# Projections over parts, wider products for the values of layer 2, and later masks in a four-layer attention kernel

## The reference

```python
# L0: LayerNorm, cross attention of 16 heads of 16, MLP 256 -> 1024 -> 256
q = (ln(x) @ q_w + q_b); k = ctx @ k_w + k_b; v = ctx @ v_w + v_b
x = softmax(q k^T / 4) v @ cproj_w + cproj_b + x;  x = x + mlp(ln(x))
# L1: queries from x; keys and values from concat([ctx, x]); key mask; RMSNorm and MLP
q = x @ q_w + q_b;  kv = concat([ctx, x], 1) @ kv_w + kv_b;  ...
# L2: two cross attentions over ctx, 16 heads of 128, one learnt key and value more per head
for j in (1, 2):
    h = ln_j(x);  qh, kh, vh = h @ wq_j + bq_j, ctx @ wk_j + bk_j, ctx @ wv_j + bv_j    # 256 -> 2048
    x = x + softmax([qh kh^T, qh bias_k] / sqrt(128)) [vh; bias_v] @ wo_j + bo_j
x = x + mlp(ln(x))                                                                     # "M2"
# L3: self attention ("L3s"), cross attention over ctx ("L3c"), 16 heads of 16, MLP
qkv = ln1(x) @ w_qkv + b_qkv;  scores = scores * mask - 10000 * (1 - mask);  ...
q = ln2(x) @ w_q + b_q;  kv = ctx @ w_kv + b_kv;  ...;  x = x + mlp(ln3(x))
```

## Time and profile before

| | us |
|---|---|
| Median of 3 runs | 1060.3 (1059.1 to 1060.75) |
| The profiled execution | 1061.92 |
| Its span (first to last instruction) | 1060.7 |
| TensorE busy | 1032.2 |
| VectorE, ScalarE, GpSimd busy | 714.9, 596.2, 601.7 |
| Idle time of TensorE in the span | 28.5 |

### The profile page before, as it was taken

How to read it: one execution, slowest core, us unless ns; L and a number is a source line. 1 busy time by engine, 2 the same in 40 slices (tenths; PEclk the granted TensorE clock), 3 DMA queues, 4 the chain that set the end, 5 groups by cost and what they waited for, 6 DMA issues and landing times.

```text
span 1060.7 us, 20845 instructions
## 1 busy us (share of the span) xinstructions
PE 1032.2 (97%) x8080; PEld 917.0 (86%) x8080; DVE 714.9 (67%) x1086; ACT 596.2 (56%) x1311; POOL 601.7 (57%) x627
## 2 busy tenths in 40 slices
PE   8999999999999999999999999999998999989988
PEld 7787888878888999999988999999998888778877
DVE  6987888899366565565567655665654378988751
ACT  6988788878633333223344223333226499999963
POOL 6874557465654344343287333553525689999860
PEclk9999999999999999999999999999999999999999
DMA  9200001000112222211130101110100000000000
...
DMA packets 33786, 40.71 MB, mean 38 GB/s; under 512 B 2111, under 2 KB 31257, under 8 KB 32025
## 3 DMA queue, kind: packets, MB, share of 16 engines
...
...
## 4 chain that ended last, share of the span: by engine, by line
PE 74%; POOL 8%; DVE 8%; ACT 5%; issue 5%; POOLq 0%; DVEq 0%; ACTq 0%
PE psum L789 14%; PE psum L683 9%; PE psum L671 8%; PE psum L803 7%; PE psum L849 7%; PE psum L709 5%; PE psum L837 5%; PE psum L817 4%; PE psum L602 4%; PE psum L699 3%; PE psum L724 2%; POOL C tile L1565 2%; PE psum L826 2%; PE psum L656 2%; ACT C tile L1364 2%
## 5 line engine op out<-in xcount | busy, mean ns | idle before, releaser
L1658 POOL TENSOR_TENSOR B tile<-B tile,B rec 128x1024 f32<-128x1024 f32 x32 | 60.8, 1899 | 204.2 <-DVE B rec L1150 204.2
L1571 POOL TENSOR_TENSOR A tile<-A tile,outer rec 128x1024 f32<-128x1024 f32 x48 | 90.7, 1897 | 74.7 <-DVE outer rec L1039 74.7
L1426 ACT ACTIVATE B own<-B max 128x8 f32<-128x8 f32 x32 | 6.7, 209 | 163.9 <-DVE B tile L1137 163.9
L1364 ACT ACTIVATE A tile<-A tile,outer min 128x128 f32<-128x128 f32 (+1 forms) x256 | 92.3, 452 | 6.1 <-DVE outer min L1032 6.0
L1282 ACT ACTIVATE B kT<-psum,B bcol 128x1024 f32<-128x1024 f32 x32 | 35.7, 1117 | 91.6 <-PE psum L789 91.6
L1364 ACT ACTIVATE C tile<-C tile,outer min 128x128 f32<-128x128 f32 x256 | 78.0, 402 | 2.1 <-DVE outer min L1032 2.1
L1178 DVE TENSOR_TENSOR x_all<-x_all,psum 128x512 f32<-128x512 f32 x64 | 42.6, 685 | 54.3 <-PE psum L849 54.3
L803 PE MATMUL psum<-B v hi,B cT hi 128*128 128x256 f32 x256 | 74.1, 289 | 0.3 <-ACT B kT L1282 0.3
L803 PE MATMUL psum<-B v hi,B cT lo 128*128 128x256 f32 x256 | 72.4, 283 | 0.0
L803 PE MATMUL psum<-B v lo,B cT hi 128*128 128x256 f32 x256 | 72.4, 283 | 0.0
L930 DVE TENSOR_SCALAR B qT<-psum,B bcol 128x1024 f32<-128x1024 f32 x32 | 41.1, 1283 | 43.3 <-PE psum L789 43.3
...
## 6 DMA issues: line engine op xcount, KB each, us to landing
...
```

The lines of the kernel that those rows point to most:

```text
L1364: i = act.activation(of_head, of_head, ACT.Exp, bias=part.min[:, u % 4, h:h + 1], scale=-1.0)
L1571: pool.tensor_tensor(tile(u, ly.nk), tile(u, ly.nk), part.rec[:, u % 4, 0:ly.per].unsqueeze(2).to_broadcast([P, ly.per, ly.nk]), ALU.mult) ...
L1658: pool.tensor_tensor(tv, tv, m.brec[:, h, :].unsqueeze(2).to_broadcast([P, B, S]), ALU.mult).then_inc(s["normalised"].sem, s["normalised"] ...
```

## The change

1. **Projections over parts.** The `k` and `v` steps of L0, all `q`, `k`, `v` of L1 and L3s, and `k`, `v` of L3c, 48 steps in all, use three fp32r products where one float32 product stood. Only the `q` of L0 and of L3c stay. `ctx` is turned straight into its two parts at the start (ScalarE copies the high one, VectorE subtracts for the low one), and the later making of them at the end of stage A goes. The inputs of L1 and L3s get parts too: in L1 the one drain becomes a copy on ScalarE and a subtraction on VectorE, in L3s VectorE writes the normalised features, ScalarE copies and GpSimd subtracts. The weights are cut by `cut_weights`, on GpSimd but for L0's keys.
2. **Where splits are made.** M2's up weights are cut in turns 1 to 4 of j = 2, the last layer's up weights in the same turns behind the second division (before: in stage C); those of L3s's q, k and v in turns 5 to 7 ahead of the second division, those of L3c's k and v in turns 5 and 6 behind it.
3. **Values of layer 2.** In turns 2 to 5 a product is one batch x four heads (512 columns) for this turn and the next, 24 of them for half of the batches. Turn 1 has 24 products of 256 columns and 24 of 512, turn 6 only 24 of 256, turns 0 and 7 the 48 of before. The values' weights are loaded and cut a turn earlier.
4. **The shift** of the normalisation in stage C is one VectorE instruction (128 x 2, two SBUF inputs) per step in place of two on GpSimd.
5. **Masks.** The cross mask is loaded behind the last values of layer 2, and its added form is made at the first scores of L3c.
6. The order tables of stages A and C are new in full.

```diff
@@ -81,6 +81,24 @@
     return 6 if turn or h else 2
 
 
+def block(turn, half):
+
+    return half if turn < 2 else (1, 0)[half] if turn % 2 else (0, 2)[half]
+
+
+def value_pieces(turn):
+
+    half = turn % 2
+    if turn == 0:
+        return [(None, 2 * n, 2, (0,)) for n in range(4)]
+    alone = [(4 + n, 2 * n + (1 - half) * 4, 2, (turn,)) for n in range(2)] if turn == 1 else []
+    if turn == NP_ - 1:
+        return [(4 + n, 2 * n, 2, (turn,)) for n in range(4)]
+    if turn == NP_ - 2:
+        return [(4 + n, 2 * n + half * 4, 2, (turn,)) for n in range(2)]
+    return alone + [(z, half * 4 + n, 1, (turn, turn + 1)) for n, z in enumerate((6, 7, 0, 1) if alone else (4, 5, 6, 7))]
+
+
 
...
+    def by_parts(event, signal, drain, weights, src, k):
+        claim(d.take(event, k), drain, event)
+        for n in range(2):
+            for c in range(C):
+                for wp, sp in PASSES:
+                    i = pe.matmul(bank(k)[:, n * T:(n + 1) * T], weights[wp][:, c, n * P:(n + 1) * P], src[sp][:, c, :],
+                                  start=(c, wp, sp) == (0, 0, 0), stop=c == C - 1 and wp == 1)
+        i.then_inc(s[signal].sem, s[signal].mark(event))
+
...
         def queries(name, k, z):
             warm((name, "q", k))
+            if name in ("L1", "L3s"):
+                wait_weights((name, "q"))
+                wait_parts((name, "in", k))
+                by_parts((name, "q", k), "q_projected", "q_drained", m.w_parts[name, "q"], (part.hi[k], part.lo[k]), z)
+                return
             wait_features((name, "in", k))
...
                 for c in range(C):
-                    i = pe.matmul(bank(z)[:, b * D:(b + 1) * D], ly.sources(m, k)[src][:, c, b * P:(b + 1) * P], ly.wv[:, c, :], start=c == 0, stop=c == C - 1)
+                    for wp, sp in PASSES:
+                        i = pe.matmul(bank(z)[:, b * D:(b + 1) * D], src[sp][:, c, b * P:(b + 1) * P], m.w_parts[name, "v"][wp][:, c, :],
+                                      start=(c, wp, sp) == (0, 0, 0), stop=c == C - 1 and wp == 1)
             i.then_inc(s["v_projected"].sem, s["v_projected"].mark(event))
...
     def values_of(j, turn, n, z):
+        _, first, batches, turns = value_pieces(turn)[n]
         if n == 0:
-            pe.wait_ge(s["wlo_made"].sem, s["wlo_made"].at((j, "v", turn)))
+            for t in (0,) if turn == 0 else (turn, turn + 1) if turn < NP_ - 2 else (turn,):
+                pe.wait_ge(s["wlo_made"].sem, s["wlo_made"].at((j, "v", t)))
         claim(z, "bv_drained", (j, turn, n))
         d.bank["v", (j, turn, n)] = z
-        for k in range(2):
+        width = len(turns) * 2 * HK
+        for k in range(batches):
...
-                                  m.cut["v"][wp][:, c, :], start=(c, cp, wp) == (0, 0, 0), stop=c == C - 1 and cp == 1)
+                    if turn == 0:
+                        w = m.cut["v"][wp][:, c, :]
+                    elif len(turns) == 2:
+                        w = m.cut_v[wp][:, c, :, :].rearrange("p t n -> p (t n)")
+                    else:
+                        w = m.cut_v[wp][:, c, turn % 2, :]
+                    i = pe.matmul(bank(z)[:, k * width:(k + 1) * width], m.bcT[cp][:, c, (first + k) * S:(first + k + 1) * S], w,
+                                  start=(c, cp, wp) == (0, 0, 0), stop=c == C - 1 and cp == 1)
         i.then_inc(s["v_projected"].sem, s["v_projected"].mark((j, turn, n)))
 
...
+
+            if (name, of) == ("L1", "in"):
+                event = (name, of, k)
+                dve.wait_ge(s["hi_drained"].sem, s["hi_drained"].at(event))
+                dve.tensor_tensor(part.lo[k][:, :, :], bank(d.bank[event]).rearrange("p (c t) -> p c t", c=C), part.hi[k][:, :, :], ALU.subtract).then_inc(
+                    s["lo_drained"].sem, s["lo_drained"].mark(event))
+                return
+            event, (scale, offset) = (name, of, k), LN[name, of]
...
+                dve.scalar_tensor_tensor(out=part.nb[k][:, :], in0=part.mv[k][:, :, 0], scalar=-1.0, in1=part.rstd[k][:, :], op0=ALU.mult, op1=ALU.mult).then_inc(
+                    s["shift_made"].sem, s["shift_made"].mark((name, of, k)))
+            elif what == "ctx":
+                k = a[0]
+                dve.wait_ge(s["ctx_hi_made"].sem, s["ctx_hi_made"].at(("ctx", k)))
+                dve.tensor_tensor(m.cT(k)[1], bank(d.bank["ctx", k]).rearrange("p (c t) -> p c t", c=C), m.cT(k)[0], ALU.subtract).then_inc(
+                    s["ctx_lo_made"].sem, s["ctx_lo_made"].mark(("ctx", k)))
+            elif what == "wcut" and tuple(a) == ("L0", "k"):
...
+                (hi, lo), raw = m.w_parts["L0", "k"], m.w_raw["L0", "k"]
+                dve.wait_ge(s["k0_hi_made"].sem, s["k0_hi_made"].at(("L0", "k")))
+                dve.tensor_tensor(lo, raw, hi, ALU.subtract).then_inc(s["k0_lo_made"].sem, s["k0_lo_made"].mark(("L0", "k")))
+            elif what == "turn_in" and (a[1] == "mlp" or tuple(a[:2]) in (("L1", "in"), ("L3s", "in"))):
+                split(*a[:3])
...
+        for k, t in enumerate(sorted(turns, key=lambda t: t % 2)):
+            width = 2 * HK
+            i = dve.tensor_tensor(m.vv[:, block(t, first // 4), first % 4:first % 4 + batches, :],
+                                  bank(d.bank["v", (j, turn, n)])[:, k * width:(k + batches) * width].rearrange("p (k d) -> p k d", k=batches),
+                                  m.bv[:, t * width:(t + 1) * width].unsqueeze(1).to_broadcast([P, batches, width]), ALU.add)
+        i.then_inc(s["bv_drained"].sem, s["bv_drained"].mark((j, turn, n)))
 
...
+    def cut_weights(name, which):
+
+        (hi, lo), raw, event = m.w_parts[name, which], m.w_raw[name, which], (name, which)
+        on, value = {"L0": ("w_v0_loaded", 16), "L1": ("w_one_loaded", 16), "L3s": ("w_c_loaded", 16 * (NP_ - 2)), "L3c": ("w_c_loaded", 16 * (NP_ - 2))}[name]
+        pool.wait_ge(s[on].sem, value)
+        pool.tensor_copy(hi, raw).then_inc(s["w_hi_made"].sem, s["w_hi_made"].mark(event))
+        pool.wait_ge(s["w_hi_made"].sem, s["w_hi_made"].at(event))
+        pool.tensor_tensor(lo, raw, hi, ALU.subtract).then_inc(s["w_lo_made"].sem, s["w_lo_made"].mark(event))
+
...
                 pool.wait_ge(s["rstd_made"].sem, s["rstd_made"].at((name, of, k)))
                 for b in range(SB):
                     shift((name, of, k, b), part.mv[k][:, b, 0:1], part.rstd[k], part.nb[k], b)
-            elif what == "turn_in" and a[1] == "mlp" and lo_signal(a[0]) == "lo_made_h":
-                lower(a[0], a[2])
+            elif what == "turn_in" and (a[1] == "mlp" and a[0] != "L1" or tuple(a[:2]) == ("L3s", "in")):
+                lower(*a[:3])
             elif what == "cut":
                 cut_up(*a)
+            elif what == "wcut" and tuple(a) != ("L0", "k"):
+                cut_weights(*a)
             elif what == "residual":
                 residual(*a)
             elif what == "scores" and units[a[0]][0].soft:
...
-            pool.wait_ge(s["v_projected"].sem, s["v_projected"].at((*last, 3)))
-        cut(j, "v", turn, ("wv_loaded", 16 * ((j - 1) * NP_ + turn + 1)))
+
+        hi, lo = (part[:, :, :] for part in m.cut["v"]) if turn == 0 else (part[:, :, turn % 2, :] for part in m.cut_v)
+        if turn == 0 and j == 2:
+            pool.wait_ge(s["weighed"].sem, s["weighed"].at((1, NP_ - 2, 1, 1)))
+        elif turn == 1:
+            pool.wait_ge(s["bv_made"].sem, s["bv_made"].at(1))
+            if j == 2:
+                pool.wait_ge(s["v_projected"].sem, s["v_projected"].at((1, NP_ - 1, len(value_pieces(NP_ - 1)) - 1)))
+        elif turn:
+            pool.wait_ge(s["v_projected"].sem, s["v_projected"].at((j, turn - 2, len(value_pieces(turn - 2)) - 1)))
+        pool.wait_ge(s["wv_loaded"].sem, 16 * ((j - 1) * NP_ + turn + 1))
+        pool.tensor_copy(hi, m.raw["v"][:, :, :]).then_inc(s["whi_made"].sem, s["whi_made"].mark((j, "v", turn)))
+        pool.wait_ge(s["whi_made"].sem, s["whi_made"].at((j, "v", turn)))
+        pool.tensor_tensor(lo, m.raw["v"][:, :, :], hi, ALU.subtract).then_inc(s["wlo_made"].sem, s["wlo_made"].mark((j, "v", turn)))
 
...
             cut_qk(2, 0)
         cut_output(j, turn)
-        if j == 2 and 2 <= turn < 5:
-            cut_up("M2", turn - 2)
+        if j == 2 and 1 <= turn < 5:
+            cut_up("M2", turn - 1)
+        if j == 2 and turn >= 5:
+            cut_weights("L3s", "qkv"[turn - 5])
         if last and j == 1:
             biases(2, 1)
             cut_qk(2, 1)
         if turn:
             divide(j, turn, 1)
-        if last and j == 2:
-            pool.wait_ge(s["bv_drained"].sem, s["bv_drained"].at((2, NP_ - 1, 3)))
-            cut_up("M2", 3)
+        if j == 2 and 1 <= turn < 5:
+            cut_up("L3c", turn - 1)
+        if j == 2 and 5 <= turn < 7:
+            cut_weights("L3c", "kv"[turn - 5])
         if last and j == 1:
             cut_values(2, 0)
             value_bias(2)
...
```

(2 more changed lines are left out.)

419 lines of the change are left out of this document (221 added, 198 removed).

## The result

The changed kernel takes 1066.4 us (median of 4 runs, 1065.2 to 1067.9) against 1059.9 before: 1.0061 times as long, 95% interval 1.0048 to 1.0075. Forecast were 1054.8, at most 1061. It is slower by 6.5 us. What happened is the rival in which VectorE bounds the last layer, beside a start that cost more than its term.

The account below looks back on a forecast made before the run. TensorE, busy 97% of the span, was taken as the bound, though not alone in mid stage C. Stage A -4.1, layer 2 +1.95 and stage C -3.3 summed to -5.5 us, from 1060.3 to 1054.8, range 1048 to 1061.

Parts of the forecast that it names:

- Projections over parts: Stages A and C: each new step saves 0.20 us, so -5.6 us in A (28 steps) and -4.0 in C (20).
- the rival in which VectorE bounds the last layer: Stage C, 900 to 1000 us: shifts and mask add 9 us to VectorE; whole 1062.6 or 1067; chance 0.13.
- a start that cost more than its term: Start of stage A: keys behind queries, scores 0 near 17.5 us, costing +1.0 us (0 to +2.9).
- I take 0.7 us of the 4.0 as lost to that and to the fuller VectorE: Stage C: shifts held by GpSimd and a fuller VectorE take 0.7 us of the 4.0 gain, leaving -3.3.
- the form in which all of it counts: Stage C, VectorE rival: all 9 us of added VectorE work lie on the path, whole 1067; rival's chance 0.13.
- GpSimd would be relieved: Stage C: argument against the VectorE rival; GpSimd has some ten us less to do in the dense stretch.
- not the 2.9 us are lost: Start of stage A: TensorE does other work meanwhile, so only warm-up products and short stretches are lost, +1.0 us.
- 4.1 us shorter: Stage A as a whole: -5.6 from projections, +1.0 for the start, +0.5 for new waits, so -4.1 us.
- +1.95: Layer 2 as a whole: 1.95 us longer, j = 1 giving -0.65 and j = 2 +2.6; matrix work alone -2.5.
- 2.63, 2.27, 0.35: Layer 2: turn 1 costs +2.63 us; turn 6 saves 2.87 less waits of 0.6 (j = 1), 2.5 (j = 2).
- VectorE's drains of the values: Layer 2: eight half-size drains replace four; cost nothing if VectorE comes free before the turn's last bank is needed.
- the mild form of one rival: Stage C, VectorE rival: half of the 9 us lies on the path, whole 1062.6; rival's chance 0.13.

Follow-up runs that it names:

- e11: Kernel before, with stage C's shift moved to VectorE as two 128x1 instructions of one SBUF input each; 1068.5 us, ratio 1.0079.
- e8: Changed kernel, with VectorE's shift as two 128x1 instructions of one SBUF input each; 1060.2 us, ratio 1.0003 to the kernel before.
- e4: Changed kernel, with L3s's three weight cuts behind GpSimd's second division in turns 5 to 7 of j = 2; ratio 1.0050 to the kernel before.
- e7: Kernel before, with L0's first keys on TensorE put behind the first queries; 1064.7 us, ratio 1.0049.
- e15: Kernel before, with nine more unused VectorE statistics instructions (3.4 us in all) at the start; 1061.0 us, ratio 1.0023.
- e17: Kernel before, with the variance plus epsilon as two 128x1 VectorE instructions instead of one 128x2; 1058.2 us, ratio 0.9987.
- e1: Changed kernel, with stage C's shift given back to GpSimd as two small instructions; 1060.3 us, ratio 1.0010 to the kernel before.
- e6: Kernel before, with only stage C's shift changed to one two-input VectorE instruction, one step behind the variance; 1075.7 us, ratio 1.0155.
- e9: Changed kernel with one-input VectorE shifts, L0's first keys and their parts ahead of turned x, GpSimd normalising streams 1, 3, 2; 1058.7 us, ratio 0.9988.
- e13: Changed kernel, with two 32-byte pads putting ctx's parts and the cut value weights at multiples of 64 bytes; ratio 1.0046 to the kernel before.

## Why the prediction was wrong

**Projections over parts: right as work, and in time only where nothing stood in the way.** At full clock TensorE's busy time up to the first division fell from 311.1 us (e11 has 311.2) to 304.5 and 304.9 (e8, e4), 6.2 to 6.7 less where 5.6 were forecast. From the last division of head 0 on it fell from between 250.4 and 250.9 (e7, e11, e15, e17) to 246.6 and 247.9 (e8, e4), 2.5 to 4.3 less where 4.0 were. In time, with the shift out of the way, stage C is 267.46 (e8) against 269.58 and 269.98 (e7, e15), 2.1 to 2.5 less: of the 4.0 some 1.5 to 2 don't come through even then, and which of the other moves takes them is open.

**Stage C failed at one step: "I take 0.7 us of the 4.0 as lost to that and to the fuller VectorE".** The price of one shift was right (0.99 us from L968's rows; 0.92 measured in the dense windows, 6.46 / 7), and so was its cause. Wrong was how much lies on the path: 6.1 us (e1), most of the 7.9 us that being held added to VectorE's work. I had this as a rival, with 0.13, in the form in which all of it counts (1067), and held against it that GpSimd would be relieved. The rival also had the wait for GpSimd's root; e8, which keeps that wait and loses nothing, shows that it wasn't needed here. In e6, where the order of VectorE's queue wasn't made for the shift, being held and the wait together cost 16 us.

**The start was mis-sized.** The step "not the 2.9 us are lost", put at +1.0 with scores 0 near 17.5, came out at 21.4, and at 19.6 to 20.3 where the clock stayed full: I saw the keys behind the queries, but not that TensorE would idle for x before them (2.7 to 4.1 us) and might drop to half its clock. e7 prices the order alone at 5.3 us in the kernel before, e15 VectorE's additions at about 2. Against a gain of 5.6 these leave stage A about where it was, and not 4.1 us shorter. Undoing the order in the changed kernel gave 1.5 us and not 5 (e9): its parts of ctx and weights, for which TensorE waits there, are a bound of their own; how much belongs to which of them wasn't separated.

**Layer 2 came near by luck, +1.95 for +2.5.** Turn 1 cost 2.75, turn 6 of j = 1 gave 1.69 and of j = 2 0.14, close to what was worked out (2.63, 2.27, 0.35). But TensorE's waits in the two turns 6 are others than forecast (timeline of TensorE: the turned weights of head 0 in j = 1, then those of head 0 and of head 1 in j = 2):

```profile
505.69 1.16 PE L897 MATMUL psum<-ident,B tile 128*128 128x128 f32 x8 [0.75 <-DVE B v L1254]
...
763.72 1.16 PE L897 MATMUL psum<-ident,B tile 128*128 128x128 f32 x8 [0.74 <-DVE B v L1254]
...
770.75 1.09 PE L897 MATMUL psum<-ident,B tile 128*128 128x128 f32 x8 [1.33 <-POOL B tile L1785]
```

In both turns 0.7 us go to VectorE's drains of the values, which I had put at nothing; behind GpSimd's second division TensorE stood 1.3 us in j = 2, not 2.5, and not at all in j = 1. e4 confirms the cut in front of the division as the cost in j = 2 (1.5 us). Turns 2 to 5 gave 0.12 and not 0.25 in j = 1, and 0.1 to 0.3 in j = 2, where I expected nothing or 0.05 more. The misplaced parts of ctx took 0.15 a turn, 1.9 us in all (e13), a cost that no view of before could show. Without it layer 2 would have been 0.6 us longer (471.08 for 470.44), a third of the forecast: an unforeseen cost made up for gains that I had taken as lost. (the earlier trace rows are of turn 3 of j = 2, not of turn 2 as the heading has it; nothing rests on that.)

The forecast missed by 11.6 us: some 5.4 are the shift, some 4 the start, the rest layer 2 and the part of stage C's gain that doesn't come through. The range's upper end took in the mild form of one rival, and these costs came together.
